# One decoder layer on one core: the two wide attentions, the joining and the first norm in one loop of 16 groups

## What is computed

```
def _mha(xq, xkv, Win, bi, Wout, bout, nh):          # nh = 4 heads of 64
    q, k, v = xq @ Win[:, :h] + bi[:h], ...          # packed in_proj
    probs = softmax(einsum('bhqd,bhkd->bhqk', q, k) / sqrt(hd))
    return einsum('bhqk,bhkd->bhqd', probs, v) ... @ Wout + bout

# in _forward (self-attention of 16 heads gives ctx)
causal_ctx = _mha(hidden_states, hidden_states, ca_Win, ca_bin, ca_Wout, ca_bout, 4)
ctx = ctx * (1.0 - CAUSAL_W) + causal_ctx * CAUSAL_W         # CAUSAL_W = 0.7
meta_ctx = _mha(ctx, ctx, mc_Win, mc_bin, mc_Wout, mc_bout, 4)
ctx = ctx * (1.0 - META_W) + meta_ctx * META_W
return ctx @ Wo + bo

x = _layernorm(x + _L0_attn_ref(x, ...))
x = _layernorm(x + _L0_xattn_ref(x, ctx_1024, ctx_1024, fside, ...))
x = _layernorm(x + _L0_ffn_ref(x, ...))
```

## Time and profile before

| | us |
|---|---|
| median of 3 runs | 3446.84 |
| lowest, highest | 3446.72, 3453.85 |
| the profiled execution | 3441.07 |
| its span in the profile | 3439.1 |

### The profile page before, as it was taken

One profiled execution on the slowest core, in us unless ns is written; L12 is line 12 of the kernel. 1 busy time (PEld: TensorE's weight loads), 2 busy tenths in 40 slices (PEclk: granted clock), 3 DMA queues, 4 the chain that ended last, 5 costly groups with the idle time before them and its releaser, 6 DMA issues. The chain is left out here.

```text
span 3439.1 us, 48449 instructions
## 1 busy us (share of the span) xinstructions
PE 2880.6 (84%) x14080; PEld 1810.3 (53%) x14081; DVE 1999.5 (58%) x2758; ACT 1409.6 (41%) x2434; POOL 970.4 (28%) x856
## 2 busy tenths in 40 slices
PE   8969999999996999958699996756888646799996
PEld 6834445454442444426444443545566445688886
DVE  5558777777772656635566664644554484333336
ACT  2306666666663434323144443422333322133335
POOL 4565610000000333333333333443000013533322
PEclk9969999999997999978799997877998777899998
DMA  7899965345414243236724423446665322323324
GB/s 242 299 248 259 274 137 72 54 63 72 60 26 95 53 95 89 63 92 209 217 53 95 98 56 104 153 151 78 91 88 85 87 64 115 116 90 128 144 109 128
DMA packets 238070, 408.69 MB, mean 119 GB/s; under 512 B 32239, under 2 KB 133463, under 8 KB 236631
## 3 DMA queue, kind: packets, MB, share of 16 engines
q1 hardware_dynamic: 209975, 323.35, 39.9%
q0 software_dynamic: 23712, 79.14, 6.8%
q10 hardware_dynamic: 4224, 4.19, 0.4%
HBM read 231.46 MB, written 175.12 MB: 118 GB/s over the span
## 5 line engine op out<-in xcount | busy, mean ns | idle before, releaser
L623 DVE TENSOR_REDUCE an_m<-an_psm 128x1 f32<-128x1024 f32 x512 | 604.6, 1220 | 188.8 <-PE an_psm L547 187.6
L603 ACT ACTIVATE an_probs<-an_pst 128x512 f32<-128x512 f32 x1024 | 533.4, 603 | 257.2 <-PE an_pst L574 256.7
L547 PE MATMUL an_psm<-an_ks,an_qs 127*128 127x512 f32 x1024 | 367.1, 443 | 39.8 <-DMA an_vs<-scr_v 30.6
L574 PE MATMUL an_pst<-an_qs,an_ks 128*128 128x512 f32 x1024 | 337.4, 408 | 11.3 <-issue 6.9
L547 PEld LDWEIGHTS an_psm<-an_ks,an_qs 127*128 127x128 f32 x1024 | 179.9, 198 | 274.4 <-issue 205.4
L559 PE MATMUL an_pacc<-an_probs,an_vs 128*32 128x512 f32 x2048 | 272.8, 604 | 11.3 <-ACT an_probs L603 11.0
L574 PEld LDWEIGHTS an_pst<-an_qs,an_ks 128*128 128x128 f32 x1024 | 192.9, 190 | 122.3 <-ACT an_probs L603 69.0
L907 ACT ACTIVATE mc_probs<-mc_pst 128x512 f32<-128x512 f32 x256 | 145.5, 597 | 248.0 <-PE mc_pst L862 247.1
L907 ACT ACTIVATE ca_probs<-ca_pst 128x512 f32<-128x512 f32 x256 | 145.7, 597 | 246.6 <-PE ca_pst L862 245.9
L862 PE MATMUL ca_pst<-ca_qs,ca_ks 128*128 128x512 f32 x512 | 171.0, 435 | 26.4 <-DMA ca_qs<-scr_cm 23.6
L862 PE MATMUL mc_pst<-mc_qs,mc_ks 128*128 128x512 f32 x512 | 167.9, 428 | 26.6 <-DMA mc_qs<-scr_mm 23.8
(11 more groups left out here) (431 smaller groups left out, 6108.0 us busy)
## 6 DMA issues: line engine op xcount, KB each, us to landing
ew_w<-scr_ws SPq DMA_DIRECT2D x10, 3072.0 KB, 13.5
scr_ws<-an_wpair POOLq DMA_DIRECT2D x27, 1024.0 KB, 5.8
an_qs<-scr_q SPq DMA_DIRECT2D x64, 256.0 KB, 11.6
an_ks<-scr_k SPq DMA_DIRECT2D x64, 256.0 KB, 13.4
ac_qs<-scr_xq SPq DMA_DIRECT2D x64, 256.0 KB, 7.7
ca_qs<-scr_cq SPq DMA_DIRECT2D x24, 512.0 KB, 8.4
ca_ks<-scr_ck SPq DMA_DIRECT2D x24, 512.0 KB, 10.2
mc_qs<-scr_mq SPq DMA_DIRECT2D x24, 512.0 KB, 8.7
```

Of the source, the lines that this page charges most:

```text
L547: last = pe.matmul(psm[:, n % 2, kh], qs[0:MROW, slot, j, q0:q0 + P], ks[0:MROW, slot, j, kh * CH:(kh + 1) * CH], start=True, stop=True)
L574: pe.matmul(pst[:, n % RING], ks[:, g, j, kc * P:(kc + 1) * P], qs[:, g, j, qh * CH:(qh + 1) * CH], start=True, stop=True).then_inc(st_rea ...
L603: act.activation(probs[:, s % 2, j], pst[:, (GH * s + j) % RING], ACT.Exp, scale=HD ** -0.5).then_inc(exp_done, 1)
L623: dve.tensor_reduce(m1[:, hq, col:col + 1], psm[:, n % 2], AX.XY, ALU.max).then_inc(mx_done, 1)
```

## The change

The stages "ca", "jo", "mc" and "ps" become one function `wide_attentions` ("wj") with one run of 16 groups, written out without a hardware loop: 8 groups of the first wide attention, then 8 of the second. A step's attention work is as before, with these differences:

- The maxima of the next group are spread evenly: one block of queries in each of the 16 steps (`units`). They have one PSUM buffer (`pm`) instead of two. On DVE the reduction of a step now stands ahead of its addition (before: behind it).
- The products with the values are done for two steps at a time, in every odd step (`values`).
- The loads of a group are issued at one place for each group (`load1`, `load0`, `loadv`), with three slots for most of the data; the maxima's rows of a group are due half a group before they are read.
- The work of "jo" and "ps" is cut into half batches of 512 tokens, c = 0 to 7, and into single PSUM tiles. The tables `JOINT` and `NORM` name the step, counted from `begin(kind, c)`, in which PE computes each tile into `pg` (2 buffers) behind its attention work. The joining of half batch c lies in group c + 2, its norm in group c + 10; those of c = 6 and 7 come after the last attention step (step 256).
- A tile of step x is evicted in step x + 1 (`answer`) by DVE, or by ACT and then DVE, ahead of that step's exponentials on ACT and ahead of its reductions and additions on DVE; what follows from it is in step x + 2 (`follow`), on DVE x + 3. A query or key tile is evicted straight into `ab`, a ring of 2 tiles (before: by ACT into `t`, by DVE and POOL into `ab`, a ring of 4).
- Between the half batches SP runs a chain of small transfers (`prepare`): row sums in, reciprocals out, reciprocals in.
- The standard deviation comes from 14 small dependent DVE instructions (`deviations`) instead of a square root on ACT.
- A `clear_semaphores` stands behind `attend_narrow`; two others go.

The diff, cut to its core:

```diff
-def attend_wide(nc, src, name):
...
-def join_attention(nc, A, scr):
...
+def wide_attentions(nc, A, scr, ident):
...
+        def units(G, s):
+            if G == 0 and s < HALF // 2:
+                return range(HALF + 2 * s, HALF + 2 * s + 2)
+            if G == NGR - 1:
+                return range(0)
+            at = HALF // 2 if G == 0 else 0
+            over = NSTEP - at
+            done = [min(NM, -(-max(0, x - at) * NM // over)) for x in (s, s + 1)]
+            return range(NM + done[0], NM + done[1])
...
+        def begin(kind, c):
+            if kind == "joint":
+                return NSTEP * (c + 2)
+            return NSTEP * (c + 2 + NKIND) if c < NCH - 1 else NSTEP * (NCH + NKIND) + LAG
+        JOINT = dict(wide=(1, 1), narrow=(2, 2), mix=(4, 5), query=(8, 9, 10, 11), value=(12, 13, 14, 15))
+        NORM = dict(wide=(1, 1), mix=(5, 6), out=(9, 10, 11, 12), turn=(15, 16), query=(19, 20))
+        work = {}
+        for c in range(NCH):
+            for kind, plan in (("joint", JOINT), ("norm", NORM)):
+                for what, steps in plan.items():
+                    for n, s in enumerate(steps):
+                        work.setdefault(begin(kind, c) + s, []).append((kind, what, c, n))
...
+            for G in range(NGR):
+                if G:
+                    store(CPB * G - 1)
+                    if G == NKIND + 2:
+                        norm_weights()
+                    if G + 1 < NGR:
+                        sp.wait_ge(pv_done, NSTEP * G)
+                        if G > 0:
+                            load1(G + 1)
+                    if G + 2 < NGR:
+                        load0(G + 2)
+                        loadv(G + 2)
+                j, o = G - 2, G - 2 - NKIND
+                if 1 <= j <= NCH:
+                    store_values(j - 1)
+                if o >= 0:
+                    load_residual(o)
+                if o >= 1:
+                    for n in range(KH):
+                        store_query("norm", o - 1, n)
+                if 0 <= j < NCH:
+                    store_joined(j)
+                if G + 1 < NGR:
+                    max_row(G + 1, 0)
+                store(CPB * G)
+                if G == 1:
+                    sp.wait_ge(self_lo, 1)
+                    for part in range(2):
+                        src = (selfhi, selflo)[part][:, 0:NSELF]
+                        sp.dma_start(scr["rself"][part].rearrange("x (k n) -> (x k) n", n=NSELF), src).then_inc(self_out, 16)
+                if 0 <= j < NCH:
+                    for n in range(4):
+                        store_query("joint", j, n)
+                if 0 <= j + 1 < NCH:
+                    prepare("joint", j + 1)
+                elif 0 <= o + 1 < NCH:
+                    prepare("norm", o + 1)
+                if o >= 0:
+                    store_norm(o)
+                if G + 1 < NGR:
+                    max_row(G + 1, 1)
+            store(BLOCKS - 1)
+            load_residual(NCH - 2)
+            for n in range(KH):
+                store_query("norm", NCH - 3, n)
+            prepare("norm", NCH - 1)
+            load_residual(NCH - 1)
+            store_norm(NCH - 2)
...
+            def values(t):
+                pe.wait_ge(exp_done, HP * (2 * t + 2))
+                x, kc = divmod(2 * t, KC)
+                slot = x // CPB % SLOT
+                if kc == 0 and x:
+                    pe.wait_ge(acc_out, x)
+                for s in (2 * t, 2 * t + 1):
+                    kc = s % KC
+                    for j in range(HP):
+                        last = pe.matmul(pacc[j * BHD:(j + 1) * BHD], vs[:, slot, kc, j * BHD:(j + 1) * BHD], probs[:, s % RING, j],
+                                         start=(kc == 0), stop=(kc == KC - 1))
+                    last.then_inc(pv_done, 1)
...
+            def attend(x):
+                G, s = divmod(x, NSTEP)
+                if s == 0:
+                    pe.wait_ge(loaded1[G % 2], 32 * (G // 2 + 1))
+                    pe.wait_ge(loadedv[G % SLOT], 16 * (G // SLOT + 1))
+                if s % KC == 0:
+                    pe.wait_ge(mrow_in[G % 2][s // KC], 16 * (G // 2 + 1))
+                todo = [divmod(n, NM) for n in units(G, s)]
+                for j in range(HP):
+                    scores(G, s, j)
+                    for ahead, n in todo[j::HP]:
+                        maxima(G + ahead, n)
+                t = x // 2
+                if s % 2 == 1 and t:
+                    values(t - 1)
+                    if t % PB == 0:
+                        row_sums(t // PB - 1)
...
+            def glue(kind, what, c, n):
+                u = nth[kind, what, c, n]
+                dst = pg[:, u % 2]
+                i = number(kind, c)
+                if u >= 2:
+                    pe.wait_ge(pg_free, u - 1)
...
+            def answer(kind, what, c, n):
+                u = nth[kind, what, c, n]
+                if what == "query":
+                    q = queries[kind, c, n]
+                    act.wait_ge(pg_ready, u + 1)
+                    if q >= ABR:
+                        act.wait_ge(ab_out[q % ABR], 16 * (q // ABR))
+                    if kind == "norm" and c == 0:
+                        act.wait_ge(w_lo, 14)
+                    elif kind == "joint" and c == 0:
+                        act.wait_ge(w_lo, 8)
+                    by = bias[:, n // KH, n % KH:n % KH + 1] if kind == "joint" else bias[:, 2, n:n + 1]
+                    act.activation(ab[:, q % ABR, 0].bitcast(FR), pg[:, u % 2], ACT.Identity, bias=by).then_inc(hi_done, 1)
...
+                for kind, what, c, n in at(x - 1):
+                    answer(kind, what, c, n)
+                for kind, what, c, n in at(x - 2):
+                    follow(kind, what, c, n)
+                if x < STEPS:
+                    for j in range(HP):
+                        act.wait_ge(st_ready, HP * x + j + 1)
+                        if x >= RING:
+                            if j == 0:
+                                act.wait_ge(pv_done, x - RING + 1)
+                            act.wait_ge(sum_done[j], adds_of(x - RING))
+                        act.activation(probs[:, x % RING, j], pst[:, j], ACT.Exp, scale=BHD ** -0.5).then_inc(exp_done, 1)
...
+                elif what == "query":
+                    q = queries[kind, c, n]
+                    by = bias[:, n // KH, n % KH:n % KH + 1] if kind == "joint" else bias[:, 2, n:n + 1]
+                    dve.wait_ge(hi_done, q + 1)
+                    dve.scalar_tensor_tensor(out=ab[:, q % ABR, 1], in0=src, scalar=by, in1=ab[:, q % ABR, 0],
+                                             op0=ALU.add, op1=ALU.subtract).then_inc(pg_free, 1)
...
+            for x in range(END):
+                for kind, what, c, n in at(x - 1):
+                    answer(kind, what, c, n)
+                for kind, what, c, n in at(x - 2):
+                    if what == "out" and n == NT - 1:
+                        deviations(c)
...
+                if x < STEPS:
+                    G, s = divmod(x, NSTEP)
+                    for ahead, n in (divmod(n, NM) for n in units(G, s)):
+                        maxima(G + ahead, n)
+                    add_up(dve, 0, x)
+                    if x % KC == 2 and x > KC:
+                        copy_out(x // KC - 1)
...
         attend_narrow(nc, scr, A, side)
-        attend_wide(nc, named(q="cq", k="ck", v="cv", m="cm", out="cout", den="cden"), "ca")
-        join_attention(nc, A, scr)
         clear_semaphores(nc)
-        attend_wide(nc, named(q="mq", k="mk", v="mv", m="mm", out="mout", den="mden"), "mc")
-        clear_semaphores(nc)
-        project_and_norm(nc, A, named(comb="comb", cout="mout", cden="mden", x1="x1", xq="xq", recip="rwide"), ident, False)
+        wide_attentions(nc, A, scr, ident)
         clear_semaphores(nc)
```

1061 lines of the change are left out of this document (532 added, 529 removed).

## The result

The changed kernel takes 3335.46 us (median of 4 runs, 3329.97 to 3341.29); the kernel before took 3450.35 us beside it. The ratio is 0.9667, with a 95% interval of 0.9645 to 0.9690: 3.3% less time. The prediction was 3308 us, with a range of 3240 to 3392. The profiled execution took 3337.19 us with a span of 3335.5, against 3439.1 in the earlier trace rows, so the span fell by 103.6 us where 138 were forecast.

What follows compares the result with a forecast made beforehand. PE was taken as the bound in the attention stages, with waits elsewhere. Start, groups, tail and barrier summed to 1062 us against 1200, 138 less, giving 3308 us, range 3240 to 3392.

Steps and rivals of the forecast that it cites:

- The wait for the query store: Joining groups: ACT's third query tile waits for the first tile's store to land, together 5.3 us a group.
- The pace without it: Joining groups laid out by pairs of steps, before the wait for the query store is added: 57.7 us a group.
- The collisions: DVE and POOL additions holding each other up; the forecast kept additions at 0.69 us on DVE, 1.28 on POOL.
- The layout by pairs: Norm group by pairs of steps: 7.6, 7.4, 9.2, 6.5, 7.2, 6.5, 5.7, 8.7, sum 58.8 us.
- Rival 2: DVE becomes the bound through POOL, each of 14 additions a group waiting 1.27 us; 3392 us, chance 0.13.
- The chain of 14: Norm group's `deviations`, 3.4 us on DVE with aggregates ahead of step 14's reduction; PE's step 15 maxima wait 2.6.
- The one buffer: Group 0: 24 blocks of maxima through a single PSUM buffer, 1.95 us each; the group 54 us.
- The last group: Group 15, counted among six norm groups at 58.8 us each.
- The tail: After step 256, two half batches with nothing to cover them: 72 us, and 3 for the barrier; bounds 50 and 90.
- The clock: PE's clock after the change: 1.0 in plain groups and low only in the tail.
- Rival 1: PE's work alone counts: joining groups 54.5 us, norm groups 52.5; the whole 3182 us, chance 0.09.
- Rival 3: Transfer chains meet bulk loads, reciprocals come about 15 us late, PE stands in 14 groups; 3519 us, chance 0.04.

Runs made afterwards that it cites:

- e1: The changed kernel with a ring of 4 query and key tiles (`ab`) instead of 2; ratio to the kernel before 0.9553.
- e9: The changed kernel with a ring of 4 tiles and POOL adding only 8 of 512 columns; ratio to the kernel before 0.9416.
- e3: The changed kernel with POOL adding only 8 of the 512 columns of its head's probabilities; ratio to the kernel before 0.9507.
- e6: The changed kernel with the standard deviation refined once instead of four times, nine small DVE instructions fewer; ratio to the kernel before 0.9591.
- e10: The changed kernel with the deviations behind the reduction and addition of step 14 instead of ahead; ratio to the kernel before 0.9659.
- e13: The changed kernel with ring of 4, two early maxima buffers, POOL halves from group 10, three refinements, deviations and normalisation behind reductions, later transposes; ratio to before 0.9497.
- e5: The changed kernel with all maxima of the first three groups alternating between two buffers, not only the first eight; ratio to the kernel before 0.9641.

## Why the prediction came out as it did

| piece | predicted | measured |
|---|---|---|
| start | 33 | 29.9 |
| group 0 | 54 | 65.4 |
| group 1 | 46.5 | 47.3 |
| joining, 8 groups | 504 | 503.8 |
| groups 10 to 15 | 349.3 | 365.2 |
| tail and barrier | 75 | 80.4 |
| sum | 1062 | 1092.0 |

The direction, the mechanism and the largest terms held; the gain was 104 us of span where 138 were forecast (115 by the ratio). The total lies in the range partly by luck, since two of the errors below cancel. Step by step:

- **The joining groups, 63.0 us, are right by luck: two errors cancel.** The wait for the query store was sized at 5.3 us; e1 measures 5.0, and its place and releaser are as forecast (6.7 us of ACT in each of eight groups), though half clock, which I had left out, is part of it. The pace without it, 57.7, was 1.9 too slow: without wait and collisions it is 55.8 (e9), above all in the pairs 4,5 and 8,9. The collisions, which I had put at nothing here, are the missing 2.2.
- **The norm groups were mis-sized by the term I left out.** The layout by pairs is right within 0.7 us in all eight once POOL's additions are short (e3: 58.1 on average, predicted 58.8). With them a group takes 64.2. Rival 2's mechanism was real and I treated it as all or nothing: I argued that in the plain pair DVE comes first, which is so (the median addition is 0.68 us), and let the late ones go uncosted. In the timeline of DVE 73 of the 192 later additions take more than 0.8 us and wait 0.73 us on average, 53 us in all; the long ones of the norm groups stand where POOL has its splits, just where DVE is late. Rival 2's price for every addition (3392) missed by 57 us, my forecast by 27.
- **The chain of 14** was sized at 2.6 us of PE's wait; it is 3.98 us and a half clock behind it. e6 shows nine of the instructions to be worth 3.6 us of one pair (group 12), twice their own length; e10 and e13 show that their place is not the cost: wherever they stand, the maxima or the transposes wait behind them.
- **Group 0** has three terms. The one buffer was costed, at 1.95 us for each of 24 blocks; in the timeline they follow one another by 2.54 us at half clock (up to 1116.5 us) and by 2.04 at the full one where nothing stands between them, and e5, with two buffers, takes 9.7 us off the group. The half clock of its first 12 us was in no term. And POOL's wait for the weights was not in my sum at all, which priced what a group repeats and left out the work that is done once. In the changed kernel it holds POOL for 17.85 us, ACT for 3.69 and PE for 2.47, and PE runs at 0.86 of the clock in the group. Group 10 pays the same kind of bill: POOL waits 7.52 us for the norm's weights, and PE 6.03 for POOL's splits of them (the last of the splits that PE's instruction waits for ends at 1744.86); the group takes 69.1 us. Timeline rows of the changed kernel:

```profile
1154.24 0.73 POOL L1089 TENSOR_SCALAR wj_bo<-wj_boraw 128x2 f32<-128x2 f32 x1 [17.85 <-DMA wj_obias<-in_L_attn_bo_dram]
...
1738.13 0.60 POOL L1074 CAST wj_w<-wj_ab 128x256 fp32r<-128x256 f32 x1 [7.52 <-DMA wj_ab<-in_L_attn_Wo_dram]
...
1744.97 0.77 PE L48 MATMUL wj_pg<-wj_cna,wj_w 128*128 128x512 f32 x1 [6.03 <-issue]
```

- **The last group** has no maxima to make and takes 44.4 us; I had costed it as a full norm group of 58.8. Without this slip in my favour the forecast would have been 14 us lower still, so what the groups with work of the norm lost to collisions, the chain and the weights is 30 us, not 16.
- **The tail** is 80.4 us with the barrier, 75 forecast. Its waits are those named (15.0 us for normalised rows, 6.5 for reciprocals, 5.0 for splits). What made the difference is not settled; e6, with the short chain, has it 5.7 us shorter (77.3 us from the last exponential to the next stage's first load, where the changed kernel has 83.0), so two chains with nothing beside them seem a good part of it; but e3, which leaves the chains alone, has it 4.5 us shorter too (78.6).
- **The clock** was to be low only in the tail. It was 0.96 in the joining groups and 0.93 in the norm groups, since PE's longer pauses were followed by stretches at half clock: between the first exponential and the last group's end PE has 20 pauses of 2.2 to 6.0 us, and the clock fell behind all but one of them (one more low stretch, 1545.9 to 1549.3, stands behind two pauses of 0.9 and 0.7). I had costed waits at their length alone.
- **Rival 1** (no limit but PE) fell: even without the store wait and POOL's additions a joining group takes 55.8 us and a norm group 58.3, against 54.5 and 52.5. **Rival 3** (the transfer chains) fell for the groups: no group shows PE waiting for the reciprocals, although the room was put at 2 us.

## What to carry to other kernels

When two engines share what their instructions need, a mean duration of before says nothing of a new order: list which instruction of one stands beside which of the other in each step, and price the coincidences where the slower engine has a backlog, not for all and not for none. A wait of PE costs more than its length if it is long enough for the clock to fall; fill or shorten the longest ones first. Work that is done once (weights, selectors) belongs in the sum: in an engine's fixed order it stands ahead of work that others wait for, and a late load there stops them all.

## What the runs showed of the hardware

- The wait of a DVE addition for POOL was never longer than the one POOL instruction beside it, also where POOL had more to do right behind it: at most 1.15, 0.61 and 0.32 us behind instructions of 1.29, 0.73 and 0.46 us, and 2.1 us behind one of 2.35.
- Not only additions of two SBUF operands are held. A change of sign on 8 columns took 1.17 us instead of 0.17, a cast of 32 columns 0.98 and a linked instruction on 4 columns 1.20 instead of 0.16; the small size is no protection. Reductions and evictions, which read PSUM, kept their durations (1.16 to 1.23 us over 252 reductions, 0.74 to 0.75 over 48 evictions of query and key tiles).
- The same pause of PE, 2.25 us at the same step of two groups of one execution, was followed by stretches at different clocks: 0.68 in group 12 and 1.00 in group 13. The pair of steps 8,9 around it takes 10.7 us in the first and 9.1 in the second, so the half clock alone costs 1.6 us there. What decided between them the trace doesn't show.

```profile
1886.60:1892.00 5.40, 5.40 (x16) 1.61 (x16) 2.46 (x2) 1.19 (x2) 4.04 (x2) 0.68 0.42 157
...
1949.30:1955.00 5.70, 5.70 (x27) 2.87 (x27) 2.50 (x4) 1.45 (x3) 3.79 (x2) 1.00 0.50 189
```
